# A fused FFN, latent attention and FFN kernel: up-projection weights stored inner axis first, another order of the first query columns, and eight output-weight loads ahead

## The reference, cut to what matters

```
x = x + 0.5 * ffn(layernorm(x))
x = x + attention(layernorm(x))
x = x + 0.5 * ffn(layernorm(x))
```

```
c_q    = h @ w_q_down                              # [512, 192]
q_nope = (c_q @ w_q_up_nope) per head              # 192 -> 32 heads x 128
q_rope = rope((c_q @ w_q_up_rope) per head)        # 192 -> 32 heads x 64
c_kv   = h @ w_kv_down ; k_rope = rope(h @ w_k_rope)     # 64 and 64 features
q_lat  = einsum('bhsd,hdr->bhsr', q_nope, w_uk)    # w_uk: [32 heads x 128, 64]
scores = (q_lat @ c_kv.T + q_rope @ k_rope.T) / sqrt(192), causal, softmax
out    = (probs @ c_kv) through w_uv [32 x 128, 64] per head, then w_out [4096, 512]
```

## Time and profile before

| | us |
|---|---|
| median of 3 runs | 1154.39 |
| lowest, highest | 1153.88, 1154.97 |
| the profiled execution | 1154.12 |
| its span in the profile | 1152.3 |
| folding (stage 3) in it | about 43 to 67 |
| first scores in it | 96.0 |

### The profile page before, as it was taken

The page is one execution under the profiler, slowest core; times in us unless marked ns, Lnnn a source line. Parts: engine busy times, 40 slices in busy tenths (PEclk is TensorE's granted clock), DMA queues, the critical chain, the costliest instruction groups (busy, mean ns, idle before and its releaser), DMA issues.

```text
span 1152.3 us, 21616 instructions
## 1 busy us (share of the span) xinstructions
PE 1092.8 (95%) x7156; PEld 891.4 (77%) x7156; DVE 908.4 (79%) x2667; ACT 607.0 (53%) x1738; POOL 705.5 (61%) x951
## 2 busy tenths in 40 slices
PE   5897999999998999999999899999999899999997
PEld 4755788888797788888788677888878678888876
DVE  4767888888676888888776888888867788888855
ACT  3554655555454655555534555555545455555542
POOL 2406877777432977777621887777723487777741
PEclk9998999999999999999999999999999999999998
DMA  9660000000101000000101000000010100000000
GB/s 285 186 195 1 1 1 1 1 1 1 38 10 65 1 1 1 1 1 1 37 1 38 37 1 1 1 1 1 1 38 28 47 2 1 2 1 2 1 2 36
DMA packets 22247, 30.94 MB, mean 27 GB/s; under 512 B 9302, under 2 KB 11094, under 8 KB 21498
## 3 DMA queue, kind: packets, MB, share of 16 engines
q1 hardware_dynamic: 19770, 24.85, 6.8%
q10 hardware_dynamic: 2368, 4.72, 1.2%
HBM read 22.23 MB, written 4.19 MB: 23 GB/s over the span
## 4 chain that ended last, share of the span: by engine, by line
PE 82%; DVE 9%; ACT 4%; issue 2%; POOL 1%; SPq 1%; DMA 1%; DVEq 0%; POOLq 0%
PE Y L992 15%; PE Y L966 13%; PE XZ L951 12%; PE Y L912 11%; PE XZ L930 6%; PE XZ L931 5%; PE XZ L932 5%; PE Y L681 4%; PE XZ L926 2%; PE XZ L681 2%; PE XZ L656 2%; DVE xT_lo L1297 1%; ACT xT_hi L1046 1%; DVE XZ L1638 1%; DVE q_turned L1580 1%
## 5 line engine op out<-in xcount | busy, mean ns | idle before, releaser
L1244 ACT ACTIVATE prob<-XZ,small 128x512 f32<-128x512 f32 (+3 forms) x512 | 266.7, 526 | 289.8 <-DVE small L1638 288.1
L637 POOL TENSOR_TENSOR prob<-prob,small 128x512 f32<-128x512 f32 (+3 forms) x512 | 361.0, 722 | 62.9 <-DVE small L1592 52.7
L1638 DVE CUSTOM_DVE_ANT_0 XZ<-XZ,mask 128x512 f32<-128x512 f32 (+3 forms) x512 | 248.0, 506 | 101.5 <-PE XZ L932 96.5
L542 POOL TENSOR_TENSOR q_sums<-q_sums,q_turned 64x512 f32<-64x512 f32 (+2 forms) x130 | 164.0, 1262 | 218.7 <-DVE q_turned L1580 217.2
L951 PE MATMUL XZ<-ident,prob 128*128 128x128 f32 x1280 | 196.0, 276 | 2.4 <-POOL prob L637 2.3
L951 PEld LDWEIGHTS XZ<-ident,prob 128*128 128x128 f32 x1280 | 150.4, 140 | 41.3 <-issue 10.3
L930 PE MATMUL XZ<-kT_hi,qT_hi 128*128 128x512 f32 (+2 forms) x384 | 148.0, 385 | 12.8 <-ACT prob L1244 9.1
L966 PE MATMUL Y<-probT,ckv 128*64 128x384 f32 (+2 forms) x1280 | 152.3, 384 | 0.0
L391 ACT ACTIVATE probT<-XZ 128x512 f32<-128x512 f32 x192 | 114.8, 598 | 64.9 <-PE XZ L951 63.9
L548 POOL TENSOR_TENSOR qT_lo<-q_sums,qT_hi 128x384 fp32r<-128x384 f32 (+2 forms) x130 | 130.1, 1001 | 23.2 <-ACT qT_hi L1211 22.7
L966 PEld LDWEIGHTS Y<-probT,ckv 128*64 128x64 f32 x1280 | 81.8, 136 | 64.2 <-issue 47.2
(11 more groups left out here) (225 smaller groups left out, 2219.7 us busy)
## 6 DMA issues: line engine op xcount, KB each, us to landing
wout_nat<-in_L_attn_w_out_dram SPq DMA_DIRECT2D x16, 512.0 KB, 4.6
out_dram<-x_sb SPq DMA_DIRECT2D x16, 256.0 KB, 2.0
x_next<-_attn_hidden_states_dram SPq DMA_DIRECT2D x12, 256.0 KB, 3.2
x_sb<-x_next SPq DMA_DIRECT2D x12, 256.0 KB, 2.3
wbase_nat<-in_L_ffn_W_base_dram ACTq DMA_DIRECT2D x1, 1024.0 KB, 5.7
x_sb<-_attn_hidden_states_dram ACTq DMA_DIRECT2D x4, 256.0 KB, 7.0
nope_a<-_L_attn_w_q_up_nope_dram ACTq DMA_DIRECT2D x1, 1024.0 KB, 5.5
rope_a<-_L_attn_w_q_up_rope_dram SPq DMA_DIRECT2D x1, 1024.0 KB, 8.0
```

Of the source, the lines that this page charges most:

```text
L542: nc.gpsimd.tensor_tensor(q, q, turned, ALU.add).then_inc(q_sum_set, 1)
L637: last = nc.gpsimd.tensor_tensor(prob[u % RING][:, c:c + w], prob[u % RING][:, c:c + w], inv_sum[:, u % RING, m:m + 1].broadcast_to([P, w] ...
L1244: last = nc.scalar.activation(prob[u % RING][:, c:c + w], score_ps[u % 2][:, c:c + w], ACT.Exp, bias=neg_max[:, u % RING, m:m + 1], scale= ...
L1638: last = nc.vector.tensor_tensor_reduce(bank, bank, mask[:, S - w:S], -1.0, HIGHEST, ALU.add, ALU.min, neg_max[:, u % RING, m:m + 1])
```

## The change

- The host hands over `w_q_up_nope` as [128 inner, 32 heads, 192] and `w_uk` as [128 inner, 32 heads, 64], each laid out inner axis first. One tile `nope_sb` takes the place of `nope_a` and `nope_b`, and the fold reads its stationary operand straight from it. The transposes and both copies are gone.
- Query folds have four banks of PSUM, not two, and the first two come ahead of the others, around the last FFN tile's low-rank part. Output fold i follows query fold i+2, not i+1. Folds 8 to 10 have a wait for the last query fold's readers.
- The first eight pairs of output weights are loaded without a wait: slots 4 to 7 have places of their own (in space that the smaller staging leaves, and that `wo_lo` takes later). Pairs 8 to 11 wait for folds 0 to 3.
- The order of the first queries on DVE, POOL and ACT is head 0 early, head 0 late, head 1 late, head 1 early. `ckT_low` of the last tile comes right behind the first part on DVE. PE still computes both early parts first; the late ones go to other banks, without a wait for DVE's reads. Units 0, 1 and 3 wait for 2, 3 and 4 parts.

```diff
-        FIRST_PARTS = ((0, EARLY), (1, EARLY), (0, LATE), (1, LATE))
+        FIRST_PARTS = ((0, EARLY), (0, LATE), (1, LATE), (1, EARLY))
+        FIRST_NEEDS = {0: 2, 1: 3, 3: 4}
...
+                def load_out(i):
+                    j = out_slot(i)
+                    if i >= SLOTS_AHEAD + SLOTS_OUT:
+                        sp.wait_ge(outw_ps, i - SLOTS_OUT + 1)
+                    elif i >= SLOTS_AHEAD:
+                        sp.wait_ge(outw_ps, i - SLOTS_AHEAD + 1)
...
                 def fold_query(g):
-                    j = g % 2
-                    pe.wait_ge(nopeTa_set, g + 1)
-                    pe.wait_ge(nopeTb_set, g + 1)
-                    if g >= 2:
-                        pe.wait_ge(fold_hi, g - 1)
-                        pe.wait_ge(fold_lo, g - 1)
+                    j = g % 4
+                    if g >= 4:
+                        pe.wait_ge(fold_hi, g - 3)
+                        pe.wait_ge(fold_lo, g - 3)
...
                 def opening_queries():            # PE
-                    for j, (head, cols) in enumerate(FIRST_PARTS):
-                        if j == 2:
-                            transpose_down(-1, STEPS - 1)
-                            pe.wait_ge(ckT_hi, ST)
-                            pe.wait_ge(ckT_lo, ST)
-                        if j >= 2:
-                            pe.wait_ge(q_rot_set, j - 1)
-                        q_products(j, 0, head, qT_ps[head], cols)
+                    for head in range(2):
+                        q_products(head, 0, head, qT_ps[head], EARLY)
+                    transpose_down(-1, STEPS - 1)
+                    pe.wait_ge(ckT_hi, ST)
+                    pe.wait_ge(ckT_lo, ST)
+                    for head in range(2):
+                        q_products(2 + head, 0, head, XZ[1][:, head, :], LATE)
...
-                    pe.wait_ge(nope_in[0], 32)
+                    pe.wait_ge(nope_in[0], 16)
+                    pe.wait_ge(uk_in, 16)
                     pe.wait_ge(prior_set, 1)
-                    transpose_nope(0, 0)
+                    fold_query(0)
                     transpose_z(-1, DOWN - 1)
+                    fold_query(1)
                     lora(-1, DOWN - 1)
...
-                    for g in range(G4):
-                        if g + 1 == G4 // 2:
-                            pe.wait_ge(nope_in[1], 32)
-                        if g + 1 < G4:
-                            transpose_nope(g + 1, (g + 1) % 2)
-                        fold_query(g)
-                        if g:
-                            fold_output(g - 1)
+                    for g in range(2, G4):
+                        if g == G4 // 2:
+                            pe.wait_ge(nope_in[1], 16)
+                        fold_query(g)
+                        fold_output(g - 2)
+                    fold_output(G4 - 2)
                     fold_output(G4 - 1)
...
                 def opening_queries():            # DVE
-                    for j, (head, cols) in enumerate(FIRST_PARTS):
-                        if j == 2:
-                            ckT_low(-1, STEPS - 1)
-                        q_rotary(j, head, 0, qT_ps[head], cols)
+                    q_rotary(0, 0, 0, qT_ps[0], EARLY)
+                    ckT_low(-1, STEPS - 1)
+                    for head in range(2):
+                        q_rotary(2 + head, head, 0, XZ[1][:, head, :], LATE)
+                    q_rotary(1, 1, 0, qT_ps[1], EARLY)
...
-                    nopeTb_copy(0, 0)
                     z_low(-1, DOWN - 1)
                     update_rows(-1, DOWN - 1)
                     for g in range(G4):
-                        if g + 1 < G4:
-                            nopeTb_copy(g + 1, (g + 1) % 2)
                         query_lo(g)
-                        if g:
-                            output_lo(g - 1)
+                        if g >= 2:
+                            output_lo(g - 2)
                         down_norms(g)
+                    output_lo(G4 - 2)
                     output_lo(G4 - 1)
```

More of the change, by code:

```diff
@@ L105, in rope_tables, with build @@
             np.ascontiguousarray(cosT), np.ascontiguousarray(np.concatenate([sinT, -sinT], axis=0)))
-def build(nc, hidden, w_q_down, w_q_up_nope, w_q_up_rope, w_kv_down, w_k_rope, w_uk, w_uv, w_out,
+def build(nc, hidden, w_q_down, nope_T, w_q_up_rope, w_kv_down, w_k_rope, uk_T, w_uv, w_out,
           W_base, b_base, lora_A, lora_B, router_W, router_b, domain_prior, active,
@@ L170, in build @@
         uk_sb = place("uk_sb", [P, H, KVL], F32, region_a)
-        nopeT_a = [place(f"nopeT_a{i}", [P, 4, P], F32, region_a) for i in range(2)]
-        nopeT_b = [place(f"nopeT_b{i}", [P, 4, 64], F32, region_a) for i in range(2)]
-        assert region_a[0] <= region_b0
+        wout_ahead = [region_b0 - SLOTS_OUT * 2 * D * 4]
+        assert region_a[0] <= wout_ahead[0]
         rb = [region_b0]
@@ L211, in build @@
         uv_nat = [place(f"uv_nat{i}", [P, 2, KVL], F32, after_outputs) for i in range(SLOTS_OUT)]
+        uv_nat += [place(f"uv_nat{i}", [P, 2, KVL], F32, uv_ahead) for i in range(SLOTS_OUT, SLOTS_AHEAD)]
         kT_top = place("kT_top", [P, P], F32, [after_outputs[0] - P * 4])
@@ L221, in build @@
         wout_nat = [place(f"wout_nat{i}", [P, 2, D], F32, fold_staging) for i in range(SLOTS_OUT)]
+        wout_nat += [place(f"wout_nat{i}", [P, 2, D], F32, wout_ahead) for i in range(SLOTS_OUT, SLOTS_AHEAD)]
         x_homes = [after_scores[0] + at for at in (4096, 12288, 6144, 14336)]
@@ L250, in build @@
         nope_in = [sem(f"nope_in{i}") for i in range(2)]
-        out_in = [sem(f"out_in{i}") for i in range(SLOTS_OUT)]
+        out_in = [sem(f"out_in{i}") for i in range(SLOTS_AHEAD)]
         ident_set, mask_set, up_zeroed, consts_set = sem("ident_set"), sem("mask_set"), sem("up_zeroed"), sem("consts_set")
@@ L433, in sequence @@
                         move(b, t)
[L435 to L441, removed]
-                                     .rearrange("(h d) r -> d h r", d=DV)).then_inc(out_in[j], 16)
-                        sp.dma_start(wout_nat[j][:], w_out[rows, :]
-                                     .rearrange("(h d) o -> d h o", d=DV)).then_inc(out_in[j], 16)
+                def load_out(i):
[4 more added lines that the diff above has]
+                        sp.wait_ge(outw_ps, i - SLOTS_AHEAD + 1)
+                    rows = bass.ds(i * (2 * DV), 2 * DV)
+                    sp.dma_start(uv_nat[j][:], w_uv[rows, :]
+                                 .rearrange("(h d) r -> d h r", d=DV)).then_inc(out_in[j], 16)
+                    sp.dma_start(wout_nat[j][:], w_out[rows, :]
+                                 .rearrange("(h d) o -> d h o", d=DV)).then_inc(out_in[j], 16)
                 def load_rope():
@@ L772, in fold_output @@
                 def fold_output(i):
-                    j = i % SLOTS_OUT
-                    pe.wait_ge(out_in[j], 32 * (i // SLOTS_OUT + 1))
+                    j = out_slot(i)
+                    pe.wait_ge(out_in[j], 32 * (1 if i < SLOTS_AHEAD else i // SLOTS_OUT))
                     if i in (0, 1):
@@ L781, in fold_output @@
                         pe.wait_ge(outw_lo, i - 2)
+                    else:
+                        pe.wait_ge(fold_hi, G4)
+                        pe.wait_ge(fold_lo, G4)
                     bank = outw_bank(i)
```

85 lines of the change are left out of this document (35 added, 50 removed).

## The result

The kernel after takes 1146.93 us in the median of 4 runs (1146.33 to 1148.09), the kernel before, timed beside it, 1154.14 (4 runs). The ratio is 0.9936 (95% interval 0.9922 to 0.9949): faster by 7.2 us. The forecast was 1146.3, range 1143.8 to 1149.8.

A forecast was written before the change was run, and what follows sets the result against it. The prediction took PE to bound the folding, with DVE close behind. Its 5.1 us from folding and 3.0 from the first queries summed to 8.1 off the profiled 1154.12, giving 1146.3 for the median, range 1143.8 to 1149.8.

The forecast's parts named there:

- Folding, 5.1: Weight folding up to the first down product: transposes removed, DVE late next; the down product comes 5.1 us earlier.
- PE's wait of 2.3 us: In the folding, PE newly waits 2.3 us, from 47.5 to 49.8, for DVE's output_lo(0) to free a bank.
- DVE's idle time at the end of 1.25: At the folding's end, the last two output folds make DVE idle 1.25 us by the walk.
- PE's 6.9 us: Seven groups of transposes in PE's chain, 6.9 us; a rival had this saving in full with the clock holding, chance 0.07.
- Part 2, 0: Down-projections after the folding: untouched, they move with the folding; gain 0.
- First queries, 3.0: First queries to DVE's mask of unit 1: reordered parts gain 3.0 us, between 2.3 and 4.0 depending on the clock.
- The gate, 0: PE's 1.05 us wait for gate_row before the first FFN product: taken as unchanged by the uk_sb load, 0.
- The bound of 1.05: Limit on the gate_row change: earlier by long uk_sb runs or later by larger nope rows, 1.05 us either way.
- that rival: gate_row comes with the shorter uk_sb load: gain 9.1 us, time 1145.3, chance 0.08.
- Loads ahead, "needed": Output-weight loads in the folding: moving them ahead is needed, as with four slots pair 4 is issued behind fold 0.
- Clock in the folding's wait: Rival: clock falls in PE's new folding wait, losing 3.4 us, 1149.7; against, slower DVE hides some; chance 0.12.
- Behind unit 4 of the first attention, 0: Everything behind unit 4 of the first attention: nothing there is touched, so no change in time.

The follow-up runs named there:

- e6: Kernel after with four more unused memsets on VectorE during the folding, one behind each of output_lo(0) to output_lo(3); 1149.75 us, ratio 0.9958 to the kernel before.
- e7: Kernel after with two more unused 512-column matmuls on TensorE behind each of fold_query(2) to fold_query(5); 1147.47 us, ratio 0.9939 to the kernel before.
- e2: Kernel after with the order and banks of the first queries as in the kernel before; 1149.53 us, ratio 0.9960 to the kernel before.
- e9: Kernel after with five and seven filler matmuls in TensorE's two waits of the first queries; 1145.39 us, ratio 0.9924 to the kernel before.
- e5: Kernel before with ScalarE's two nope-weight loads issued at 18.7 us and not at 11.3; 1152.99 us, ratio 0.9986 to the kernel before.
- e1: Kernel before with only w_uk laid out inner axis first; 1154.88 us, ratio 1.0002 to the kernel before.
- e3: Kernel after with four pairs of output weights loaded ahead, not eight (SLOTS_AHEAD = 4); 1146.93 us, ratio 0.9937 to the kernel before.
- e4: Kernel after with w_uk in its old layout in memory; 1147.64 us, ratio 0.9940 to the kernel before.
- e10: Kernel after with nine and five filler matmuls in TensorE's waits at the start of the last steps; 1146.12 us, ratio 0.9928 to the kernel before.

## Why the prediction was right in its time, and where it was wrong

- **Folding, 5.1.** 4.77 in the profile. The mechanism is the one that was walked: PE's wait of 2.3 us was 2.11, DVE's idle time at the end of 1.25 was 0.40 and 0.81, and e6 and e7 show that DVE's work, and not PE's, sets the end. The error is 0.3 us. That PE's 6.9 us did not all come through is this change of the bound, not a loss.
- **Part 2, 0.** The first queries are 5.92 earlier, the same as the first down product: 0.
- **First queries, 3.0.** 2.70 in the profile, and e2 puts it at 2.6. The late products moved by 1.69 (1.72 was forecast), unit 0 by 2.18 (2.3). From unit 0 to the mask of unit 1 it was 5.47, between the 6.0 of half clock and 4.3 of full; e9 measured the latter, 4.33, with the clock held.
- **The gate, 0.** This is the step that failed: 1.05 of the 1.15 us gained by the last FFN update are its wait. The bound of 1.05 had it, but for a shorter load of `uk_sb`; larger rows of the nope weights were named only for bringing `gate_row` later. e5 shows that their load is what holds it up, and in the form of the kernel after it doesn't. The reason given for 0 was a misreading too: 348 GB/s was taken to show no loss by short rows, and with long rows the same window moves 389. The Trainium skill, DMA: Bandwidth & Descriptors, Specifications, gives 512 bytes as the least size for full rate. In the rate the traces agree with it (348 and 389 GB/s for 256-byte and for long rows). By the use that the prediction made of it, e1, which turns the 256-byte rows into long ones, should have been 1.05 us faster; its ratio is 1.0002, and the wait is still there. The size of the gain came out as that rival said, for another reason.
- **Loads ahead, "needed".** Wrong, but at no price: e3 with four slots takes the same time. Eight pairs do not keep the queues busy until about 47 either: the window from 42 to 43 us moves 304 GB/s, that from 43 to 44 61.
- **Clock in the folding's wait.** The rival priced a fall there at 3.4 us. It did not fall in the kernel after, and fell in e5 without such a wait. In e4 it fell right behind the wait, and the stage took 0.20 us longer: DVE, which sets the end, hides nearly all of it, as the prediction's "against" had it.
- **Behind unit 4 of the first attention, 0.** The edits touch nothing there, and so it was put at nothing; 0.86 us was lost at the second attention, to the clock and to a late copy.

In sum 1.15 + 4.77 + 2.70 - 0.86 = 7.76, against 8.1. Two errors of about 1 us, the gate and the second attention, cancel, and so the time of 1146.3 is closer than its parts. That is luck: a fall of the clock like this one is in some profiles and not in others. By the medians the gain is 7.2 us.

## What to carry to other kernels

When the engine that is the whole chain loses work, count the busy time of the next one in the same stretch and walk its order by hand: here this gave the gain within 0.3 us, and the end under another order within 0.1. A wait for tiny loads can end with the landing of a large load on another queue, so a change in the large load's shape is to be costed where the small ones are waited for. Where every stage begins with a gap of one or two us, a microsecond of gain can be lost again, to the clock or to a copy that lands late; compare profiles instruction by instruction, before a stage is blamed.

## What the runs showed of the hardware that was not expected

- Filling PE's idle times of 1.5 and 2.1 us with matmuls kept the granted clock at 1.00, where it was 0.50 for 3.4 us (e9), and at the last steps, where it was 0.50 for nearly 7 us (e10). In the profiles it saved 1.15 us from unit 0 to the mask of unit 1, and 0.55 from the last output's addition to the second tile's update at the end.
- With the same idle times ahead of it (1.24 to 1.26 and 0.35 to 0.37 us), the clock fell in one execution and not in another: at the second attention in the kernel after and in e5, and not in the kernel before and e3.
- A copy of 256 KB took 2.3 us from issue to landing at the second attention of the kernel before, and 4.0 at that of the kernel after. A store of 256 KB took 2.0 us there in both, and one took 4.2 in e9.
- 256-byte rows in one of the loads of a stretch went with 348 GB/s over the stretch, long rows in it with 389.
